# Moving the four PSUM copies of a head's relative scores from VectorE to ScalarE

## The reference, cut to what matters

```
dist = r[None, :] - r[:, None];  idx = clip(dist, -64, 64) + 64
rk, rv = embK[idx], embV[idx]
logits = einsum('bhqd,bhkd->bhqk', q, k) + einsum('bhqd,qkd->bhqk', q, rk)
w = softmax(logits, axis=-1)
out = einsum('bhqk,bhkd->bhqd', w, v) + einsum('bhqk,qkd->bhqd', w, rv)
```

## Time and profile before

| | before |
|---|---|
| median of 3 runs | 4418.2 us (4414.44 to 4430.01) |
| profiled execution, its own time | 4430.09 us |
| its span, first to last instruction | 4428.4 us |
| mean granted TensorE clock | 0.941 |
| busy over the span: PE / DVE / ACT / POOL | 90% / 79% / 68% / 33% |
| `rel_attention`, first relative matmul to last `weigh` | 145.1 to 2034.2 us |

### The profile page before, as it was taken

The page is one execution under the profiler, slowest core; times in us unless marked ns, Lnnn a source line. Parts: engine busy times, 40 slices in busy tenths (PEclk is TensorE's granted clock), DMA queues, the critical chain, the costliest instruction groups (busy, mean ns, idle before and its releaser), DMA issues. The chain is left out here.

```text
span 4428.4 us, 77243 instructions
## 1 busy us (share of the span) xinstructions
PE 4001.6 (90%) x26592; PEld 2106.5 (48%) x26592; DVE 3490.8 (79%) x6304; ACT 2991.0 (68%) x5821; POOL 1445.9 (33%) x1405
## 2 busy tenths in 40 slices
PE   7699999999999999996879999999999996689997
PEld 4344444444444444443533333333333332589997
DVE  6688888888888888862769888988888881577775
ACT  3067777777777777783218888888888884256664
POOL 0255666666666656662100000000000000613222
PEclk9589999999999999998959999999999997689998
DMA  7656666666666767654662323233333302666664
GB/s 269 179 142 164 150 163 161 163 154 168 155 159 159 168 159 165 161 116 129 234 120 40 54 30 54 40 44 45 44 44 46 43 13 70 176 207 174 177 170 115
DMA packets 486195, 556.39 MB, mean 126 GB/s; under 512 B 60260, under 2 KB 426836, under 8 KB 476524
## 3 DMA queue, kind: packets, MB, share of 16 engines
q1 hardware_dynamic: 465980, 526.94, 49.1%
q0 software_dynamic: 19824, 24.52, 3.5%
HBM read 347.67 MB, written 206.76 MB: 125 GB/s over the span
## 5 line engine op out<-in xcount | busy, mean ns | idle before, releaser
L1096 ACT ACTIVATE ra_p<-ra_psS 128x512 f32<-128x512 f32 x2048 | 1089.6, 605 | 368.2 <-PE ra_psS L1173 266.1
L370 DVE TENSOR_REDUCE pa_pm<-pa_psA 128x2 f32<-128x1024 f32 x1024 | 1208.3, 1219 | 140.7 <-PE pa_psA L459 140.7
L1007 DVE TENSOR_REDUCE ra_pm<-ra_psA 128x1 f32<-128x896 f32 x1024 | 1113.5, 1087 | 205.9 <-PE ra_psA L1131 190.4
L433 ACT ACTIVATE pa_p<-pa_psS 128x512 f32<-128x512 f32 x2048 | 1063.5, 604 | 249.4 <-PE pa_psS L484 245.0
L484 PE MATMUL pa_psS<-pa_qs,pa_zs 50*128 50x512 f32 x2048 | 793.4, 464 | 77.3 <-ACT pa_p L433 62.8
L459 PE MATMUL pa_psA<-pa_zs,pa_qs 48*128 48x512 f32 x2048 | 797.2, 472 | 44.2 <-DMA pa_zs<-k_halves 23.8
L1131 PE MATMUL ra_psA<-ra_zs,ra_qs 48*128 48x512 f32 x2048 | 736.0, 455 | 44.9 <-DVE ra_pm L1009 23.8
L1173 PE MATMUL ra_psS<-ra_qs,ra_zs 50*128 50x512 f32 (+3 forms) x2176 | 713.8, 411 | 32.4 <-ACT ra_p L1096 17.5
L484 PEld LDWEIGHTS pa_psS<-pa_qs,pa_zs 50*128 50x128 f32 x2048 | 342.2, 185 | 626.2 <-ACT pa_p L433 606.7
L1204 PE MATMUL ra_psO<-ra_p,ra_vs 128*32 128x512 f32 (+3 forms) x6400 | 566.6, 459 | 0.0
L495 PE MATMUL pa_psO<-pa_p,pa_vs 128*32 128x512 f32 x4096 | 548.0, 607 | 0.0
(11 more groups left out here) (247 smaller groups left out, 4977.9 us busy)
## 6 DMA issues: line engine op xcount, KB each, us to landing
relative_rows<-ra_rst SPq DMA_DIRECT2D x128, 512.0 KB, 4.0
ra_blk<-window_rows SPq DMA_DIRECT2D x128, 512.0 KB
mo_w_raw<-ffn_W SPq DMA_DIRECT2D x58, 1024.0 KB, 5.5
ra_zs<-k_halves SPq DMA_DIRECT2D x192, 248.0 KB, 7.4
ra_dl<-relative_rows SPq DMA_DIRECT2D x128, 256.0 KB, 5.4
window_rows<-ra_pc SPq DMA_DIRECT2D x128, 256.0 KB, 4.8
pa_qs<-q_halves SPq DMA_DIRECT2D x192, 128.0 KB, 6.3
pa_zs<-k_halves SPq DMA_DIRECT2D x192, 128.0 KB, 6.9
```

Source lines behind the costliest of these rows:

```text
L370: dve.reduce_max(pm[:, par, 2 * a:2 * a + 2], psA[w][:, :, :], AX.X).then_inc(s_am.h, 1)
L433: act.activation(pr[:, i % NPR, :], psS[:, slot(i), :], ACT.Exp).then_inc(s_ex.h, 1)
L1007: dve.reduce_max(pm[:, q, i, 2 * left:2 * left + 1], psA[w][:, lo:lo + 2 * G - P], AX.X).then_inc(s_far.h, 1)
L1096: act.activation(dst, psS[:, slot(i), :], ACT.Exp if kind == "E" else ACT.Copy).then_inc(s_cp.h, 1)
```

## The change

All four chunks of a head, listed in `R_ACT`, are copied by a new ScalarE `keep_r`. VectorE keeps its turn list but skips the R entries. The one semaphore `s_rc`, which counted copies in order, becomes four, one per chunk, and every waiter (SyncE's `write_r`, TensorE's `released` and its start list) waits on the chunk's own.

```diff
+R_ACT = (0, 1, 2, 3)
...
+    r_by = {REL_LEAD + NR * R_STEPS[c] // STEPS + before_o - 1: c for c in R_ACT}
...
+        s_rc = [sem(f"s_rc{c}") for c in range(4)]
...
-                s_rc.wait(engine, 4 * (t + 2) + a + 1)
+                s_rc[a].wait(engine, t + 3)
...
-                s_rc.wait(sp, 4 * t + c + 1)
+                s_rc[c].wait(sp, t + 1)
...
-                        if not real(t, kind, a):
+                        if not real(t, kind, a) or kind == "R" and a in R_ACT:
...
+            def keep_r(t, c, w):
+                s_r.wait(act, 4 * t + c + 1)
+                s_rw[(c - 2) % 4].wait(act, 16 * (t + (c >= 2)))
+                act.activation(rst[:, c % 2, :], psA[w][:, :], ACT.Copy).then_inc(s_rc[c].h, 1)
+
+            for c in R_ACT:
+                keep_r(0, c, first.index(("R", c)) % 2)
             s_init.wait(act, NINIT)
             for j in early:
                 window_exp(0, 0, j)
+            for c in R_ACT:
+                keep_r(1, c, first.index(("R", 4 + c)) % 2)
...
                         copy_out(t + i // NR, i % NR)
+                        if i in r_by and t + 2 < HEADS:
+                            keep_r(t + 2, r_by[i], (PT + body.index(("R", r_by[i]))) % 2)
                         if i in evac_after:
                             evacuate(t, evac_after[i])
```

More of the change, by code:

```diff
@@ L664, in rel_attention @@
             ("s_a", "s_far", "s_am", "s_nm", "s_mt", "s_mh", "s_mr", "s_mq"))
-        s_r, s_rc, s_ms, s_rm = (sem(n) for n in ("s_r", "s_rc", "s_ms", "s_rm"))
+        s_r, s_ms, s_rm = (sem(n) for n in ("s_r", "s_ms", "s_rm"))
+        s_rc = [sem(f"s_rc{c}") for c in range(4)]
         s_rw, s_rr, s_pw, s_pr = ([sem(f"{n}{c}") for c in range(4)] for n in ("s_rw", "s_rr", "s_pw", "s_pr"))
@@ L1025, in keep_r @@
                 s_rw[(c - 2) % 4].wait(dve, 16 * (t + (c >= 2)))
-                dve.tensor_copy(rst[:, c % 2, :], psA[w][:, :]).then_inc(s_rc.h, 1)
+                dve.tensor_copy(rst[:, c % 2, :], psA[w][:, :]).then_inc(s_rc[c].h, 1)
             def split_m(t, w):
@@ L1050, in _ @@
                 elif kind == "R":
-                    keep_r(a // 4, a % 4, n % 2)
+                    if a % 4 not in R_ACT:
+                        keep_r(a // 4, a % 4, n % 2)
                 else:
@@ L1214, in _ @@
                     elif was == "R":
-                        s_rc.wait(pe, b + 1)
+                        s_rc[b % 4].wait(pe, b // 4 + 1)
                     else:
```

## The result

The changed kernel takes 4521.9 us (median of 4 runs, 4518.05 to 4526.33) against 4424.1 for the kernel before beside it: a ratio of 1.020, with a 95% interval of 1.017 to 1.023. It is slower by 98 us, and the forecast of 4436 (4408 to 4468) missed it. Two executions that ran far slower at a much lower clock (one of the kernel before, one of `e10_busy_s3`) are left out of every median.

A forecast was written before the change was run, and what follows sets the result against it. VectorE was taken to bound steps 1 to 4 of a head. Terms +33 (loop), +4 (start) and -20 (clock) sum to +17 us: 4447 against the profiled execution, 4435 against the median, rounded up to 4436, range 4408 to 4468.

The forecast's parts named there:

- The copy: ScalarE's 128x1024 copy from PSUM, one per R chunk: taken as 1.04 us, range 1.0 to 1.21.
- Steps 1 and 2: A head's first two steps, cut at each `weigh`, with the R0 and R1 copies: no change in time.
- Step 3: R2's copy stands ahead of the `psO` evacuation and five copies in ScalarE's queue: +1.0 us per head (+0.5 to +1.4).
- Step 4: R3's copy goes ahead of a window exponential and copy 26 on ScalarE: +0.1 us per head (-0.5 to +0.4).
- The clean head: A head at clock 1.00 throughout: near 56.2 us after the change, 55.10 before.
- the queue's term: Loss in the head loop from ScalarE's queue: 30 x (1.0 + 0.1) = +33 us, from 0 to +54.
- the start: Ahead of the loop, head 1's first R copy comes behind eleven exponentials: +4 us, once (2 to 5).
- granted clock: Slow-clock time over heads 1 to 29, mostly in step 5, 43 us before: -20 us (-43 to +14).
- half as often: Assumed frequency of clock falls after the change, against before: the basis of the -20 us.
- The worst case: Clock falls once more in every fifth head, at 2.35 us (5.84 - 3.49): 14 us lost.
- Step 5 and later: nothing: From a head's fifth step on, TensorE and ScalarE stand as before: no change; growth there would show the forecast wrong.
- the clock gives nothing back: Rival: TensorE stalls in steps 3 and 4, no slow-clock time returns: +37 us, 4455, or 4469 with 14 more; chance 0.34.

The follow-up runs named there:

- e10_busy_s3: Changed kernel with TensorE kept at work in step 3 alone (fill 23 repeated six times over): 4463.0 us, 30 over the kernel before, ratio 1.0064.
- e1: Changed kernel with only chunks R0 and R1 copied by ScalarE, R2 and R3 by VectorE as before: 4452.6 us, ratio 1.0026 to the kernel before.
- e8: Changed kernel with TensorE repeating fill 23 six times over in step 3 and fill 28 three times over in step 4: 4427.5 us, ratio 0.9997.
- e11: Changed kernel with TensorE kept at work in step 4 alone (fill 28 three times over): 4532.2 us, 99 over the kernel before, ratio 1.0205.
- e5: Changed kernel with ScalarE evacuating `psO` before it copies R2 in step 3: 4528.4 us, 98 over the kernel before, ratio 1.0219.
- e4: Changed kernel with TensorE repeating fill 23 four times in step 3 and fill 28 once in step 4: 4489.4 us, ratio 1.0103 to the kernel before.

## Why the prediction missed

Right were the steps of ScalarE's queue. The copy takes 1024 ns (1.04 taken). Steps 1 and 2 cost nothing: 4.06 and 5.12 us, and e1 shows it. Step 3 was to end 1.0 us late (+0.5 to +1.4) and does, at 4.75; every link is in the timeline above (copy, evacuation and five copies starting 0.92 and 0.48 apart, the fill that waited 1.81 us). Step 4 was to cost +0.1; at full clock it takes 4.16 against 4.13 (e10). The clean head was put at 56.2 and takes 56.15 (e8; no head of the changed kernel keeps its clock). Over 29 heads the queue's term is 29 x (56.15 - 55.10) = 30 us, near the sum's 1.1 per head.

Too high was the start: the first `weigh` stands at 237.28 against 236.42, 0.9 us and not 4 late, since head 0's exponentials themselves began 2.7 us earlier (197.02, not 199.75) and let the R copies behind them in:

```profile
197.02 4.49 ACT L1106 ACTIVATE ra_sw<-ra_sw,ra_nm 128x256 f32<-128x256 f32 x11
201.42 1.91 ACT L1118 ACTIVATE ra_rst<-ra_psA 128x1024 f32<-128x1024 f32 x2
```

Head 0 took 2.0 us longer. With the 0.9 ahead of it and the 90.0 of heads 1 to 29 that is all but 0.3 of the 93.2 us.

The step that failed is the **granted clock**: -20 us, "half as often", with +14 as the worst. Heads 1 to 29 take 1730.67 us, 59.68 each; 59.68 - 56.15 = 3.53 is lost to the clock per head, 102 us in all, against 43 before. The term is +59, and 30 + 59 is the 90 us by which these heads grew (1730.67 - 1640.63). Sign and size were both wrong:
- How often. The sum had the shifted timing halve the falls. But the earlier trace rows showed a step 4 with 0.9 us of idle TensorE ahead of a slow step 5 (it is so in 14 of 29 heads), and the working itself put a second stall into step 3, which came out at 1.37 us of 4.75. Nothing in those rows spoke for fewer falls, and a second stall was a reason for more. The count went from 15 to 29 of 29 heads.
- How much. The worst case priced a fall at 2.35 us, that of one slow step 5, though the 43 us before are 2.8 for each of 15 falls. Behind step 3 a fall takes step 4 along (5.02 us in head 14, 4.16 at full clock), step 5 (4.73 against 3.49), and in 13 heads step 6, so that it costs 3.5 on average. "Step 5 and later: nothing" held for the queues alone: at full clock step 5 takes 3.49 as before (e8), and the clock made it grow, which the prediction had named as a sign of being wrong.
- Its cap. The rival "the clock gives nothing back" had the mechanism, the place and the argument for it, but its worst was a fall "once more in every fifth head".

That the clock is a cause and not a witness is shown by e8, e10 and e11: with TensorE at work in the stalls, the loss goes while ScalarE's queue and the steps at full clock stay as long. The rule of the Trainium skill's page Perfetto Trace Analysis, section Matmul Optimizations, that TensorE scales its power with utilization, agrees with these runs; weighed by it, the added stall was a loss to expect.

The Trainium skill's page Perfetto Trace Analysis, section Optimizing Scalar/DVE Operations, says that offloading some work to Scalar may make sense where VectorE is saturated. Here it brought no gain: VectorE's busy time fell by 4.3 us a head (48.77 to 44.48; 4.9 forecast), and no step of a clean head got shorter by more than 0.02 us (e8).

## What to carry to other kernels

Before work is moved to an engine with idle time, look at what stands behind it in that engine's queue and who waits for that: 1.03 us placed ahead of five awaited copies made a step longer by as much. Where a stall of TensorE is followed by a lower granted clock, as here, don't count on fewer falls from an added stall, and price a fall over all the slow steps behind it. And look for such stalls in the kernel as it is: filling one with repeated matmuls that nobody needs gave 1.1%.

## What was not expected of the hardware

- Useless work paid: four repeated fills a head took the clock's falls from 15 of 29 heads to none and 44 us off the kernel before.
- The clock's losses outlast their cause: behind a step 3 with 1.37 us of idle TensorE, steps 4 and 5 ran at 0.58 and 0.72 although TensorE was busy almost all through them (4.76 of 5.02 and 4.73 of 4.73 us), and a mean head lost 3.5 us.
- The falls in step 4 go with the idle time of step 3 by degrees: with TensorE idle there for 1.37 us (changed kernel), 0.89 (e5), 0.45 (e4) and 0.01 (e10), the clock in step 4 was below 0.9 in 29, 15, 8 and 1 of 29 heads. Heads with a fall anywhere were 29, 28, 27 and 15, so where e5 and e4 kept step 4 clean, the fall mostly came behind it. Why one head falls and the next with the same steps doesn't wasn't settled.
